# Two added products of 512 columns per group in the two attention passes of a four-layer graph network

## What is computed

```python
# layer 0, relation attention, for each edge type r of 4
rel_t = lrelu(concat(x[src], x[tgt]) @ W_R[r] + b_R[r])
e = lrelu(concat(rel_t @ W_Q[r] + b_Q[r], rel_t @ W_K[r] + b_K[r]) @ a_w + a_b)
attn = segment_softmax(e where edge_type == r, tgt)
h = h + segment_sum((rel_t @ W_V[r] + b_V[r]) * attn, tgt)
...
# layer 2, 8 heads of 16
a = einsum('eho,eho->eh', (k[src] @ rel_att), q[dst]) * rel_pri / sqrt(16)
attn = segment_softmax(a, dst)
h_agg = segment_sum((v[src] @ rel_msg) * attn, dst)
```

## Time and profile before

| | |
|---|---|
| median of 3 runs | 3276.14 us (3275.95 to 3276.39) |
| profiled execution | 3281.18 us |
| its span | 3279.4 us |
| granted TensorE clock, mean of the span | 0.645 |
| PE busy | 2154.2 us (66%) |
| POOL busy | 2044.5 us (62%) |
| DVE busy | 1683.5 us (51%) |
| relation pass, first gather to last L715 | 107.6 to 790.8 us |
| head pass, first gather to last L1755 | 1661.0 to 2279.4 us |

### The profile page before, as it was taken

One profiled execution on the slowest core, in us unless ns is written; L12 is line 12 of the kernel. 1 busy time (PEld: TensorE's weight loads), 2 busy tenths in 40 slices (PEclk: granted clock), 3 DMA queues, 4 the chain that ended last, 5 costly groups with the idle time before them and its releaser, 6 DMA issues. The chain is left out here.

```text
span 3279.4 us, 47591 instructions
## 1 busy us (share of the span) xinstructions
PE 2154.2 (66%) x10935; PEld 1873.2 (57%) x10935; DVE 1683.5 (51%) x5452; ACT 945.0 (29%) x3043; POOL 2044.5 (62%) x1817
## 2 busy tenths in 40 slices
PE   5458888876859999995646666776535555555530
PEld 3357777765748888885435556666434444444430
DVE  3367777775123333334526666667664444444426
ACT  2356666652124444442200000000012222222210
POOL 3577776730017777772157777770548888888883
PEclk9655555555559999997765555555666666666655
DMA  5655544420513333331044444440035555555545
GB/s 212 234 147 146 144 137 135 138 78 17 193 49 91 89 90 90 90 92 37 37 130 133 131 133 137 135 134 12 12 81 80 80 78 79 79 79 79 79 52 180
DMA packets 322945, 340.02 MB, mean 104 GB/s; under 512 B 118323, under 2 KB 240880, under 8 KB 321466
## 3 DMA queue, kind: packets, MB, share of 16 engines
q0 software_dynamic: 113152, 163.68, 24.3%
q1 hardware_dynamic: 209626, 174.53, 17.8%
HBM read 264.10 MB, written 75.48 MB: 104 GB/s over the span
## 5 line engine op out<-in xcount | busy, mean ns | idle before, releaser
L2352 POOL DMA_INDIRECT side<-e_merged,e_row x416 | 649.4, 1561 | 142.7 <-issue 107.3
L655 POOL DMA_INDIRECT e_gathered<-rel_src_table,rel_idx x416 | 436.3, 1049 | 203.3 <-issue 121.2
L1696 POOL DMA_INDIRECT e_kv<-kv_table,e_idx x416 | 421.4, 1013 | 126.0 <-issue 124.9
L434 POOL DMA_INDIRECT e_gathered<-msg_src_table,e_idx x416 | 399.6, 961 | 125.7 <-issue 116.2
L1223 ACT COPY e_spread<-e_ps_t 32x128 f32<-32x128 f32 x832 | 212.0, 255 | 375.4 <-PE e_ps_t L2262 350.2
L2262 PE MATMUL e_ps_t<-ident,e_onehot 128*128 128x128 f32 x104 | 46.7, 451 | 389.9 <-DVE e_onehot L1215 389.9
L1743 PE MATMUL e_ps_q<-e_window,e_spread 64*128 64x128 f32 x832 | 214.6, 437 | 111.5 <-DMA e_window<-q_table 72.2
L712 PE MATMUL e_ps_a<-e_typed,e_rel 128*128 128x72 f32 x832 | 206.0, 429 | 98.9 <-DVE e_typed L836 98.9
L698 PE MATMUL e_ps_r<-e_window,e_spread 64*128 64x128 f32 x832 | 215.3, 437 | 67.0 <-DMA e_window<-rel_dst_table 37.9
L1743 PEld LDWEIGHTS e_ps_q<-e_window,e_spread 64*128 64x128 f32 x832 | 185.0, 325 | 127.2 <-DMA e_window<-q_table 93.8
L2262 PEld LDWEIGHTS e_ps_t<-ident,e_onehot 128*128 128x128 f32 x104 | 18.3, 176 | 416.9 <-DVE e_onehot L1215 416.9
(11 more groups left out here) (419 smaller groups left out, 4658.3 us busy)
## 6 DMA issues: line engine op xcount, KB each, us to landing
e_src_all<-src_padded SPq DMA_DIRECT2D x104, 256.0 KB
e_keys<-tile_keys SPq DMA_DIRECT2D x104, 128.0 KB
e_window<-rel_dst_table SPq DMA_DIRECT2D x416, 32.0 KB
e_offsets<-group_offsets SPq DMA_DIRECT2D x104, 128.0 KB
e_attr<-in_edge_attr_dram SPq DMA_DIRECT2D x103, 128.0 KB
rel_src_table<-t_up SPq DMA_DIRECT2D x5, 2560.0 KB
n_parts<-side SPq DMA_DIRECT2D x40, 320.0 KB
side<-n_zeros SPq DMA_DIRECT2D x48, 256.0 KB
```

What stands on the lines that cost most here:

```text
L434: pool.indirect_dma_start(to[:, u, j, :], None, table, bass.IndirectOffsetOnAxis(ap=numbers[:, half, u * J + j:u * J + j + 1], axis=0)).th ...
L655: pool.indirect_dma_start(gathered[:, q % GS, j, :], None, rel_table, bass.IndirectOffsetOnAxis(ap=rel_idx[:, q * J + j:q * J + j + 1], ax ...
L1696: pool.indirect_dma_start(kv[:, slot, j, :], None, kv_table, bass.IndirectOffsetOnAxis(ap=idx[:, half, k * J + j:k * J + j + 1], axis=0)). ...
L2352: pool.indirect_dma_start(side[copy], bass.IndirectOffsetOnAxis(ap=row[:, s4, j:j + 1], axis=0), merged[:, s4, j, :], None, compute_op=ALU ...
```

## The change

A helper `keep_warm` issues products with weights `ident` (128 by 128) and moving operand `iota` (512 columns) into a PSUM bank of their own, `ps_warm`. Nothing waits for them, they wait for nothing but their turn on PE, and nobody reads the bank. Two of them follow the expansion in every iteration of both PE programs, also in the iterations at the end that expand nothing.

```diff
+    def keep_warm(pe, spare, times):
+        for _ in range(times):
+            pe.matmul(spare, ident[:, :], iota[:, 0:spare.shape[-1]], start=True, stop=True, skip_group_check=True)
...
@@ rel_pass
+            ps_warm = psum("ps_warm", [P, 512])
...
                 for t in range(Q + AHEAD + 1):
                     c, late = divmod(t - 3, CH)
                     if t < Q:
                         expand(t)
                     if late == 0 and 1 <= c <= NCH:
                         rows(c - 1)
+                    keep_warm(pe, ps_warm[:, :], 2)
                     if late == 1 and 1 <= c <= NCH:
                         columns(c - 1)
                     if 0 <= t - AHEAD < Q:
                         total_up(t - AHEAD)
...
```

## The result

| | before | after |
|---|---|---|
| median of 5 runs | 3275.95 us (3275.28 to 3276.39) | **3297.66 us** (3290.92 to 3306.96) |
| profiled execution | 3281.18 us | 3290.92 us |
| its span, mean granted clock | 3279.4 us, 0.645 | 3289.2 us, 0.785 |
| relation pass, first gather to last totals | 107.6 to 790.8 us | 108.5 to 782.5 us |
| head pass, first gather to last totals | 1661.0 to 2279.4 us | 1649.7 to 2291.4 us |

The ratio is 1.0069, 95% interval 1.0048 to 1.0090: slower by 22 us where 16 us of gain were forecast. The profiled run of after is the shortest of its five. In the two profiles the relation pass is 9.2 us shorter (683.2 to 674.0), the head pass 23.3 us longer (618.4 to 641.7), and all that has no edit is 4.4 us shorter together; the cause of that is not known.

The account below looks back on a forecast made before the run. PE at 1.2 GHz paced the groups of both passes, with softmax stalls and POOL's gathers as further bounds; relation pass -30 and head pass +14 gave -16 us, 3276.1 to 3260 us, own range 3232 to 3269.

Parts of the forecast that it names:

- the last rival: Both passes: weight loads keep the low pace, relation group 5.1 us, head group 4.6, +145 us, 3421 us; chance 0.03.
- The ends: Groups of totals alone closing each pass: 18 in the relation pass cost +6 us, 13 in the head pass +11.
- the group at the high clock: One PE group with its pair at 2.4 GHz: 4.2 us in the relation pass, 3.75 in the head pass.
- near the lower end: Group times chosen near full halving (4.15 and 3.67 us), not the 0.58 factor (4.54 and 3.98).
- 11 groups: -7.3 us: Relation pass, per block: some 11 groups at 4.2 us for 4.86 give -7.3 us.
- -1.7: Head pass, per block: 11 groups at 3.75 us for 3.90 give -1.7 us.
- the first group after the stall: First group after each softmax, still low: +2.6 us per relation block, +3.0 per head block.
- six block intervals: Relation pass: block gain counted over six intervals, -40 us, of which POOL's room lets pass about 36.
- -6.7: Relation pass: sum of the terms per block, -6.7 us, leaving 70.6 us a block.
- the pair costs more than the clock gives back: Rival, placed in the head pass's groups: head pass +35, relation pass -8, together +27, 3303 us; chance 0.17.
- its condition: Rival's deciding test: a head group at the high clock passes 3.90 us, its own 16 instructions taking over 2.18 us.
- POOL's room of 37 us: Relation pass: gathers take 557 us spread over 594, so 37 us of room caps the gain.

Follow-up runs that it names:

- burst_pair: The change plus three further products in PE's stall at every softmax of both passes: 3243.78 us against 3279.43 for the kernel before, ratio 0.9892.
- burst_ramp4: Repeat of burst_ramp in a batch where the kernel before took 3275.33 us: 3215.96 us, ratio 0.9818.
- burst_mix: burst_pair with one product per head-pass group and none behind groups without an expansion: 3224.81 us against 3279.43 for the kernel before, ratio 0.9841.
- rel_only: The change with its pairs in the relation pass alone: 3971.86 us against 3951.29 for the kernel before, ratio 1.0048.
- rel_only2: Repeat of rel_only in another batch: 3270.81 us against 3279.43 for the kernel before, ratio 0.9983.
- head_only: The change with its pairs in the head pass alone: 4007.68 us against 3951.29 before, ratio 1.0138; repeated in another batch 3298.86 against 3279.43, ratio 1.0062.
- burst_ramp: burst_mix with pairs behind the first three groups of each head block, one product behind the others: 3988.99 us against 3937.14 before, ratio 1.0136.

## Why the prediction was wrong

**Held.** The clock rises with two products a group, within one or two groups after each stall, and stays up until the next softmax: 0.87 and 0.84 were measured, "about 0.85" forecast. Products with the identity as weights raised it, so the rule on transposes of the Trainium skill (TensorE: Matmul & The Clock Gate, its part on PE-mode transpose) does not reach these ordinary products, as I had argued. The weight loads do not keep the low pace either: eight instructions of L718, each with a 128-column load, follow each other in 0.94 us for 1.92. The prediction's remark on the load time that the Trainium skill gives (TensorE: Matmul & The Clock Gate, section on LDWEIGHTS), that by it the last rival would be right, was a slip. By that page 128 columns over 1.2 GHz are some 107 ns a load, which makes an estimate of 0.85 us for eight; that fits into the 0.98 us of the earlier trace rows and the 0.94 us here, so the pace contradicts nothing there. The load records themselves are longer and do shorten: those of the totals of the head pass have a median of 333 ns in before and 192 ns in the change. The ends: +6.6 us for +6 in the relation pass, +10.9 for +11 in the head pass.

**Failed: the group at the high clock**, taken at 4.2 and 3.75 us "near the lower end". Measured 4.38 and 3.83. The pair was set at 1.72 us and takes 1.82 from start to start; the relation group's own instructions take 2.56 us for the 2.48 set, those of the head group 2.01 for 2.03. The step "11 groups: -7.3 us" is 11 x 0.48 = -5.3; in the head pass "-1.7" is 11 x 0.07 = -0.8.

**Failed: the first group after the stall**, set at +2.6 and +3.0 us on the thought that part of its pair is already high. All of it is low (3.71 and 3.57 us): with the other terms as they are, the relation block's -3.9 (78.6 to 74.7) leaves +3.4 for it, the head block's +1.8 (73.3 to 75.1) leaves +3.4 too. Taking it away in burst_pair gave 3.0 and 3.0. In two of the relation blocks a second group ran low, which costs 3.5 us (78.2 for 74.7).

**Failed: "six block intervals".** The last of the six is no full one: in it the expansions run out, and three pairs already stand behind totals alone, which cost 0.4 us each where 0.66 was to be won. It also has one of the two second low groups. It went from 71.6 to 74.0 us.

**The sum.** Relation pass: the intervals changed by -2.2, -3.0, -4.1, -4.0, -3.7, -0.5 and +2.4 us, -15 together where -36 was to come; with +6.6 at the end and 0.8 less ahead of the first block it is -9 where -30 stood. By terms, the last six intervals gave -13 against the -40 of six times -6.7: 0.18 us in each of some 63 groups, 11, are lost to the dearer group, 0.8 x 6 = 5 to the first group, 2 x 3.5 = 7 to the second low ones, 3 x 1.1 = 3 to the three groups without an expansion; 1 is left, in the interval of 75.7 us. Head pass: 7 x 1.8 + 10.9 = +23 where +14 stood. So what came is the rival "the pair costs more than the clock gives back" in its place and in nearly its size in the relation pass (-8), with less in the head pass (+23 for +35), but not by its condition: a head group at the high clock stayed below 3.90 us. The 0.07 us won on each of 11 groups could not pay for one low group, +3.4. POOL's room of 37 us, which I had taken as the cap, was never reached.

The median lies a further 7 us above the profiled run, and nothing in the forecast speaks of that; see the last section.

## What to carry over

Products that only raise the clock must be paid out of what the clock gives back to the group's own instructions: here 2.3 us of 4.86 and 1.9 us of 3.90 against a pair of 1.82 us at the high and 3.7 us at the low clock, with nothing to win where few instructions of one's own remain. Put them where the engine stands anyway, just ahead of the work behind a stall (burst_pair: from +22 to -36 us), use the full dose only until the clock is up and half of it to hold, and leave them out of ends that do not pay (18 us here). Together that gave -59 us (burst_ramp4). Then look which engine is next: here POOL's gathers, 5.4 us a group.

## What the runs showed of the hardware

Where the clock changes level in the middle of a pass, the run times can spread. The kernel before spreads by 0.03% over the five runs beside the change (by up to 0.25% in the two other batches near 3276 us, over more runs), the changed one by 0.5%: 3290.92, 3293.61, 3297.66, 3303.38 and 3306.96 us with mean granted clocks of 0.785, 0.785, 0.782, 0.779 and 0.780. burst_mix ran from 3222.34 us (0.757) to 3269.45 us (0.745), and its trace shows how: a block takes 61.5 or 95.1 us. burst_pair, in which nearly every first group is high, spreads by 0.1%. That the change's other runs had more second low groups is likely from their clocks, but is not shown: their traces were not taken.

In the five long batches the kernel before took 3934 to 3951 us. It need not be the chip: one whose number came up in two batches was there with 3275 and with 3934 us. The two traces of one program, rel_only and rel_only2, show where the time goes. Of the 703 us between them 264 lie in the relation pass, 179 between the two passes and 260 in the head pass; all behind the head pass takes 998 to 999 us in both. The granted clock of the untouched head pass is 0.50 in both, and a single instruction takes what it takes elsewhere (L1763: 421 ns in the median); the groups stretch because engines stand. VectorE's waits in the head pass of rel_only, from 2250 to 2900 us, are led by

```profile
DVE parts L1848 <- remote: 198.0, 24, 12.8
DVE e_spread L1806 <- DMA e_offsets<-group_offsets: 71.3, 7, 10.4
```

and in that of rel_only2, from 1680 to 2280 us, by

```profile
DVE parts L1848 <- PE e_ps_a L1763: 87.4, 97, 1.6
DVE e_spread L1806 <- DMA e_offsets<-group_offsets: 74.0, 12, 10.8
```

The figures are us in total, times, and the longest. rel_only has 24 stalls of up to 12.8 us that the trace puts down to "remote", which rel_only2 has not got. The added products cost more in the long batches (rel_only 1.0048 for 0.9983, head_only 1.0138 for 1.0062), and burst_ramp, 0.9818 of before in the other kind, is slower than before there (1.0073 to 1.0136). What stands behind these stalls is open; what gains beside a kernel of 3276 us need not gain beside one of 3940.
